# Routing of tokens to experts: maxima made earlier, running sums on TensorE, two multiplications on ScalarE and GpSimd

## The reference

```python
gate_logits = jnp.einsum('bsd,dn->bsn', x, Wg) + bg
gate_weights = jax.nn.softmax(gate_logits, axis=-1)
topv, topi = jax.lax.top_k(gate_weights, TOPK)          # 2 of 8
h = jax.nn.gelu(jnp.einsum('bsd,ndh->nbsh', x, W1) + b1[:, None, None, :], approximate=False)
h = jax.nn.gelu(jnp.einsum('nbsh,nhf->nbsf', h, W2) + b2[:, None, None, :], approximate=False)
eo = jnp.einsum('nbsf,nfd->nbsd', h, W3) + b3[:, None, None, :]
comb = jnp.sum(jax.nn.one_hot(topi, NE, dtype=x.dtype) * topv[..., None], axis=-2)
out = jnp.einsum('nbsd,bsn->bsd', eo, comb)
```

## Time and profile before

| | before |
|---|---|
| runs, us | 1767.7, 1780.8, 1783.01 |
| profiled execution, us | 1767.65 |
| its span, us | 1765.9 |
| TensorE busy | 1422.5 us, 81% |
| VectorE busy | 975.9 us, 55% |
| ScalarE busy | 614.0 us, 35% |
| GpSimd busy | 418.3 us, 24% |
| mean granted TensorE clock | 0.933 |

### The profile page before, as it was taken

One profiled execution on the slowest core, in us unless ns is written; L12 is line 12 of the kernel. 1 busy time (PEld: TensorE's weight loads), 2 busy tenths in 40 slices (PEclk: granted clock), 3 DMA queues, 4 the chain that ended last, 5 costly groups with the idle time before them and its releaser, 6 DMA issues. The chain is left out here.

```text
span 1765.9 us, 29494 instructions
## 1 busy us (share of the span) xinstructions
PE 1422.5 (81%) x9331; PEld 878.0 (50%) x9331; DVE 975.9 (55%) x2623; ACT 614.0 (35%) x1389; POOL 418.3 (24%) x588
## 2 busy tenths in 40 slices
PE   2466888888888986399999993568888875899997
PEld 1234555555555553155656562345555543566554
DVE  5456666666666652522222223367878752567775
ACT  0122444434444443022222231335555542232231
POOL 2233223322223200111111103454555420000000
PEclk9878999999999998599999996789999997899999
DMA  3245344533444310651111102664555420200000
GB/s 89 58 50 66 47 60 53 64 51 54 54 53 56 45 24 9 233 180 68 32 35 34 33 25 55 172 119 103 113 110 118 98 51 20 72 1 13 12 1 25
DMA packets 165337, 112.77 MB, mean 64 GB/s; under 512 B 32690, under 2 KB 155826, under 8 KB 165056
## 3 DMA queue, kind: packets, MB, share of 16 engines
q1 hardware_dynamic: 150272, 99.04, 27.7%
q0 software_dynamic: 3408, 9.31, 2.2%
q10 hardware_dynamic: 11504, 2.53, 0.8%
HBM read 46.48 MB, written 12.45 MB: 33 GB/s over the span
## 5 line engine op out<-in xcount | busy, mean ns | idle before, releaser
L892 ACT ACTIVATE first_probs<-pair 128x512 f32<-128x512 f32 x320 | 190.3, 597 | 302.6 <-PE pair L408 273.4
L449 DVE TENSOR_REDUCE first_negmax_x<-bank 128x2 f32<-128x512 f32 x256 | 177.0, 692 | 109.5 <-PE bank L393 96.1
L1885 ACT ACTIVATE second_probs<-pair 128x512 f32<-128x512 f32 x192 | 113.8, 598 | 129.2 <-PE pair L408 112.6
L393 PE MATMUL bank<-kept_stack_cross 96*128 96x256 bf16 x768 | 150.4, 277 | 9.7 <-DMA kept_stack_cross<-second_parts_x_q 7.9
L408 PE MATMUL pair<-kept_stack_cross 98*128 98x256 bf16 x768 | 148.8, 276 | 1.5 <-DMA kept_stack_cross<-second_rows_x 1.0
L1439 PE MATMUL pair<-kept_w,experts_hidden_t 128*128 x312 | 141.5, 596 | 0.0
L386 PE MATMUL bank<-kept_mask_q,kept_ident 128*128 128x512 bf16 x256 | 99.3, 388 | 35.0 <-DVE first_negmax_x L449 26.8
L449 DVE TENSOR_REDUCE second_negmax_x<-bank 128x2 f32<-128x512 f32 x128 | 88.5, 692 | 60.2 <-PE bank L393 52.2
L393 PEld LDWEIGHTS bank<-kept_stack_cross 96*128 96x128 bf16 x768 | 74.1, 101 | 74.3 <-issue 21.2
L1480 ACT ACTIVATE experts_hidden_t<-bank,kept_b 128x128 f32<-128x128 f32 x156 | 44.4, 367 | 187.4 <-PE bank L1414 187.4
L1394 POOL DMA_INDIRECT experts_expert_rows<-x_mid,kept_row_of x39 | 36.9, 947 | 276.4 <-PE bank L1406 250.3
(11 more groups left out here) (430 smaller groups left out, 2974.1 us busy)
## 6 DMA issues: line engine op xcount, KB each, us to landing
kept_stack_self<-first_parts_a SPq DMA_DIRECT2D x128, 64.0 KB, 5.6
kept_w<-in_L_ffn_W SPq DMA_DIRECT2D x16, 512.0 KB, 7.5
kept_w<-in_L_ffn_W SPq DMA_DIRECT2D x8, 1024.0 KB, 7.0
kept_stack_self<-second_parts_a SPq DMA_DIRECT2D x128, 64.0 KB, 3.4
kept_stack_cross<-first_parts_x_k SPq DMA_DIRECT2D x96, 64.0 KB
kept_stack_cross<-first_parts_x_q SPq DMA_DIRECT2D x96, 64.0 KB
kept_stack_cross<-second_parts_x_k SPq DMA_DIRECT2D x96, 64.0 KB
kept_stack_cross<-second_parts_x_q SPq DMA_DIRECT2D x96, 64.0 KB
```

What stands on the lines that cost most here:

```text
L393: mm = pe.matmul(out, q, k, start=mask is None, stop=True, skip_group_check=True)
L449: return dve.tensor_reduce(negmax[:, 2 * n:2 * n + 2], bank[:, :].rearrange("p (m t) -> p m t", t=D), AX.X, ALU.max, negate=True)
L892: act.activation(probs[i % RING][:, :], key_bank[i % 2][:, :], ACT.Exp, scale=att.scale).then_inc(probs_made, 1)
L1885: act.activation(probs[i % RING][:, :], key_bank[i % 2][:, :], ACT.Exp, scale=att.scale).then_inc(probs_made, 1)
```

## The change

Per batch, `keep_logits` of the first layer now also makes the maxima and their indices. In routing, the counts per expert over all batches are summed by 16 products of 8 columns that add into the same columns of a bank, and the ranks (earlier rows and earlier batches) by 16 products of 128, 120, ... 8 columns; the doubling steps go. The running ends of tiles come from an 8 x 8 comparison table, a product and a sum. The 0/1 table of tiles is kept apart as `hot`; ScalarE multiplies it by the row number, GpSimd by the batch number, both into `in_tile`. The owners' steps stand behind the second comparison by row. The shares and the integer slots are made at the start of VectorE's list in the expert stage. Kept between stages now: `best`, `best_at`, `weight`, `share` and `slot_numbers`.

```diff
@@ keep_logits, first layer
                 dve.tensor_tensor(t["logits"][:, b, :], small_bank[:, 0:NE], t["bg"][:, :], ALU.add).then_inc(logits_kept, 1)
+                dve.drain()
+                dve.max(t["best"][:, b, :], t["logits"][:, b, :])
+                dve.drain()
+                dve.max_index(t["best_at"][:, b, :], t["best"][:, b, :], t["logits"][:, b, :])
@@ route_tokens, gpsimd
+            by_tile = [P, 2, B, TILES]
+            pool.wait_ge(iotas_made, IOTAS)
+            pool.wait_ge(hot_made, 1)
+            pool.tensor_tensor(in_tile[:, 1, :, :, :], hot[:, :, :, :], ids_b[:, :, :].unsqueeze(3).broadcast_to(by_tile), ALU.mult).then_inc(ids_b_made, 1)
@@ tensor
             pe.wait_ge(chosen_made, 1)
+            for b in range(B):
+                mm = pe.matmul(ps[1][:, 0:NE], t["ones_bf"][:, :], chosen16[:, b, :], start=(b == 0), stop=(b == B - 1))
+            mm.then_inc(counted, 1)
             flat = chosen16[:, :, :].rearrange("p b e -> p (b e)")
-
-            pe.matmul(ps[0][:, 0:P], t["before16"][:, :], flat, start=True, stop=True)
-            pe.matmul(ps[1][:, 0:P], t["ones_bf"][:, :], flat, start=True, stop=True).then_inc(counted, 1)
-            pe.wait_ge(in_tile_made, 1)
+            for step in range(B):
+                mm = pe.matmul(ps[0][:, step * NE:B * NE], t["ones_bf"][:, :] if step else t["before16"][:, :], flat[:, 0:(B - step) * NE],
+                               start=(step == 0), stop=(step == B - 1), skip_group_check=True)
+            mm.then_inc(ranked, 1)
+            pe.wait_ge(ids_p_made, 1)
+            pe.wait_ge(ids_b_made, 1)
@@ scalar
-            act.activation(share[:, :], gap[:, :], ACT.Exp).then_inc(weight_made, 1)
+            act.activation(share[:, :], gap[:, :], ACT.Exp)
+            act.wait_ge(iotas_made, IOTAS)
+            act.wait_ge(hot_made, 1)
+            act.activation(in_tile[:, 0, :, :, :].rearrange("p n b c -> p (n b c)"), hot[:, :, :, :].rearrange("p n b c -> p (n b c)"), ACT.Copy, scale=ids_p[:, 0:1])\
+                .then_inc(ids_p_made, 1)
@@ vector: maxima, indices, shares and doubling steps removed (...), now
+            dve.wait_ge(iotas_made, IOTAS)
+            dve.tensor_tensor(choice[:, :, :, :], iota8[:, :].unsqueeze(1).unsqueeze(1).broadcast_to(by_choice),
+                              first_second[:, :, :].unsqueeze(3).broadcast_to(by_choice), ALU.is_equal)
+            dve.drain()
+            dve.tensor_tensor(chosen16[:, :, :], choice[:, 0, :, :], choice[:, 1, :, :], ALU.add).then_inc(chosen_made, 1)
+            dve.tensor_tensor(below[:, :, :], iota8[:, :].unsqueeze(2).broadcast_to([P, NE, NE]), iota8[:, :].unsqueeze(1).broadcast_to([P, NE, NE]), ALU.is_gt)
...
             dve.wait_ge(counted, 1)
+            dve.tensor_scalar(tiles[:, :], ps[1][:, 0:NE], float(P - 1), 1.0 / P, ALU.add, ALU.mult)
...
+            dve.tensor_tensor(before_of[:, :, :], below[:, :, :], tiles[:, :].unsqueeze(1).broadcast_to([P, NE, NE]), ALU.mult)
+            dve.drain()
+            dve.tensor_reduce(base[:, :], before_of[:, :, :], AX.X, ALU.add)
+            dve.drain()
+            dve.tensor_tensor(ends[:, :], base[:, :], tiles[:, :], ALU.add)
             dve.tensor_scalar(base[:, :], base[:, :], float(P), None, ALU.mult)
             dve.drain()
+            dve.wait_ge(ranked, 1)
+            dve.tensor_tensor(place[:, :, :], ps[0][:, 0:P].rearrange("p (b e) -> p b e", e=NE), base[:, :].unsqueeze(1).broadcast_to([P, B, NE]), ALU.add)
+            dve.drain()
+            dve.tensor_tensor(choice[:, :, :, :], choice[:, :, :, :], place[:, :, :].unsqueeze(1).broadcast_to(by_choice), ALU.mult)
+            dve.drain()
+            dve.tensor_reduce(slots[:, :, :], choice[:, :, :, :], AX.X, ALU.add)
...
+            dve.tensor_tensor(hot[:, :, :, :], iota_t[:, :].unsqueeze(1).unsqueeze(1).broadcast_to(by_tile),
+                              tile_of[:, :, :].unsqueeze(3).broadcast_to(by_tile), ALU.is_equal).then_inc(hot_made, 1)
             dve.scalar_tensor_tensor(within[:, :, :], tile_of[:, :, :], -float(P), slots[:, :, :], ALU.mult, ALU.add)
-            dve.tensor_tensor(in_tile[:, 1, :, :, :], in_tile[:, 0, :, :, :], ids_b[:, :, :].unsqueeze(3).broadcast_to(by_tile), ALU.mult)
-            dve.drain()
-            dve.tensor_scalar(in_tile[:, 0, :, :, :], in_tile[:, 0, :, :, :], ids_p[:, 0:1], None, ALU.mult).then_inc(in_tile_made, 1)
+            dve.drain()
             for n in range(2):
                 dve.tensor_tensor(in_row[:, n, :, :], iota_p[:, :].unsqueeze(1).broadcast_to(by_row),
                                   within[:, n, :].unsqueeze(2).broadcast_to(by_row), ALU.is_equal).then_inc(in_row_made, 1)
+            dve.tensor_tensor(reached[:, :, :], iota_t[:, :].unsqueeze(2).broadcast_to([P, TILES, NE]),
+                              ends[:, :].unsqueeze(1).broadcast_to([P, TILES, NE]), ALU.is_ge)
+            dve.drain()
+            dve.tensor_reduce(owner[:, :], reached[:, :, :], AX.X, ALU.add)
+            dve.drain()
+            dve.tensor_scalar(t["owner"][:, :], owner[:, :], float(NE - 1), None, ALU.min)
             dve.wait_ge(listed, 1)
@@ run_experts, vector, ahead of the first copy_rows
+            dve.tensor_reduce(total[:, :], t["weight"][:, :, :], AX.X, ALU.add)
+            dve.memset(t["slots"][:, :, B:], 0)
+            dve.tensor_copy(t["slots"][:, :, 0:B], t["slot_numbers"][:, :, :])
+            dve.drain()
+            dve.reciprocal(t["shares"][:, 0, :], total[:, :])
+            dve.drain()
+            dve.tensor_tensor(t["shares"][:, 1, :], t["share"][:, :], t["shares"][:, 0, :], ALU.mult)
             copy_rows(0)
```

More of the change, by code:

```diff
@@ L1190, in route_tokens @@
         sb, sem = open_tensors(nc, ctx, "route")
-        best, best_at = sb("best", [P, B, 8]), sb("best_at", [P, B, 8], U32)
         first_second = sb("first_second", [P, 2, B])
         less = sb("less", [P, B, NE])
-        weight = sb("weight", [P, B, NE])
-        total, gap, share = sb("total", [P, B]), sb("gap", [P, B]), sb("share", [P, B])
-        choice = [sb(f"choice_{n}", [P, B, NE]) for n in range(2)]
+        weight, share, slots = t["weight"], t["share"], t["slot_numbers"]
+        gap = sb("gap", [P, B])
+        choice = sb("choice", [P, 2, B, NE])
         chosen16 = sb("chosen16", [P, B, NE], BF16)
[L1198 to L1201, removed]
+        place = sb("place", [P, B, NE])
+        tiles, ends, base = (sb(n, [P, NE]) for n in ("tiles", "ends", "base"))
+        below, before_of = (sb(n, [P, NE, NE]) for n in ("below", "before_of"))
         iota8, iota_t = sb("iota8", [P, NE]), sb("iota_t", [P, TILES])
@@ L1262, in _ @@
         def _(dve):
[L1263 to L1271 removed]
+            logits, best, best_at = t["logits"], t["best"], t["best_at"]
+            by_choice, by_tile, by_row = [P, 2, B, NE], [P, 2, B, TILES], [P, B, P]
             for n in range(2):
@@ L1304, in _ @@
             dve.drain()
-            dve.tensor_copy(ends[:, :], tiles[:, :])
-            at, other = ends, ends2
-            for step in (1, 2, 4):
-                dve.drain()
-                dve.tensor_tensor(other[:, step:], at[:, step:], at[:, :NE - step], ALU.add)
-                dve.tensor_copy(other[:, 0:step], at[:, 0:step])
-                at, other = other, at
+            dve.tensor_tensor(before_of[:, :, :], below[:, :, :], tiles[:, :].unsqueeze(1).broadcast_to([P, NE, NE]), ALU.mult)
@@ L1312, in _ @@
             dve.drain()
-            dve.tensor_tensor(base[:, :], at[:, :], tiles[:, :], ALU.subtract)
-            dve.tensor_tensor(reached[:, :, :], iota_t[:, :].unsqueeze(2).broadcast_to([P, TILES, NE]),
-                              at[:, :].unsqueeze(1).broadcast_to([P, TILES, NE]), ALU.is_ge)
-            dve.tensor_tensor(place[:, :, :], run[now][:, :, :], counts[:, :, :], ALU.subtract)
+            dve.tensor_reduce(base[:, :], before_of[:, :, :], AX.X, ALU.add)
             dve.drain()
-            dve.tensor_reduce(owner[:, :], reached[:, :, :], AX.X, ALU.add)
+            dve.tensor_tensor(ends[:, :], base[:, :], tiles[:, :], ALU.add)
@@ L1328, in _ @@
             dve.drain()
-            for n in range(2):
-                dve.tensor_reduce(slots[:, n, :], choice[n][:, :, :], AX.X, ALU.add)
-            dve.drain()
-            dve.memset(t["slots"][:, :, B:], 0)
-            dve.tensor_copy(t["slots"][:, :, 0:B], slots[:, :, :])
             dve.tensor_scalar(tile_of[:, :, :], slots[:, :, :], 0.5 * P - 0.5, 1.0 / P, ALU.subtract, ALU.mult)
@@ L2585, in program @@
             ("wd_t", [P, KT, LAT], F32), ("absorbed_t", [P, KT, P], F32), ("wuv_t", [P, D], F32), ("wo1_t", [P, KT, D], F32),
-            ("logits", [P, B, NE], F32), ("slots", [P, 2, B + 2], I32), ("shares", [P, 2, B], F32), ("owner", [P, TILES], I32), ("row_of", [P, TILES], I32),
```

(1 more changed line is left out.)

47 lines of the change are left out of this document (8 added, 39 removed).

## The result

The changed kernel takes 1765.21 us, the median of 22 runs (1762.44 to 1774.42). The kernel before, run as often, takes 1775.43 us (1762.74 to 1784.71). The ratio is 0.9949, with a 95% interval of 0.9933 to 0.9965: some 9 us faster, between 6 and 12 (the two medians themselves lie 10.2 us apart). That is within 1%, as forecast, and on the forecast's side; but the sum said 3.1 us, and the 1777 us of the forecast are 12 us above the measured median. The profiled execution of the changed kernel took 1765.42 us (span 1763.6, mean clock 0.924), against 1767.65 (1765.9, 0.933).

The account below looks back on a forecast made before the run. Routing (26.2 of 1765.9 us) delays a TensorE-paced expert stage, so its end is paid in full. Routing -4.36, later start +0.55, first layer +0.7 give -3.1 us from the median 1780.8: about 1777 us, range 1760 to 1785.

Parts of the forecast that it names:

- the 0.55 that it adds at the end: Last batch of the first layer: its index search has no cover, so routing starts 0.55 us later.
- the hold: First comparison by row: VectorE with two SBUF inputs is blocked by GpSimd's product until 725.44, 2.41 us.
- The front: Routing's start: 3.46 us come off nominally, but almost nothing is gained, as the matmuls stand behind the b12 transposes.
- The narrow products: Routing's count and rank matmuls on TensorE: taken as 0.065 us apart, with bounds of 0.03 and 0.29.
- The 22.4 us that the prediction gives as a sign: Stage from first weight issue to first gather would take about 22.4 us instead of 26.2.
- One step came right by luck: After routing: nothing later uses up the gain, as SP has issued the first weights by 724.6, nine microseconds before the gather.
- The term for the first layer (+0.7): First layer: index searches delay reductions TensorE waits for; cost between 0 and 1.4 us, taken as 0.7.
- VectorE was held: Rival, comparisons by row: no hold between the engines, rows start at 723.03, sum -5.5 us, 1775; chance 0.2.
- GpSimd finished at 725.86 and not after the second comparison: Rival: GpSimd loses the race twice, multiplies after both comparisons by row, 727.5 to 730.0; -1.7 us, 1779; chance 0.15.
- the index search cost nothing that shows: Rival, first layer: each batch's index search delays reductions TensorE needs, up to 9.3 us; +5.5 us, 1786; chance 0.12.
- a narrow product took 0.027 us and not 0.29: Rival, routing's counts and ranks: narrow products cost 0.29 us each, slots at about 727.1; +3.4 us, 1784; chance 0.04.
- The one that the first layer moves by ten: Rival: the first layer falls into another pattern of waits and moves ten or more us either way; chance 0.1.

Follow-up runs that it names:

- experiment 3: Changed kernel with the place within the tile (`within`) in PSUM instead of SBUF; 1762.29 us, 0.9933 of the kernel before, routing 19.1 us.
- experiment 4: Changed kernel with TensorE's wait for the bias rows and their eight transposes put behind the rank products; 1760.57 us, 0.9925 of the kernel before, routing 17.6 us.
- exp. 5: Changed kernel with both `within` in PSUM and the bias transposes behind the rank products; 1762.56 us, 0.9941 of the kernel before, routing 15.5 us.
- experiment 1: Kernel before with only the maxima and indices moved to each batch's logits; 1773.12 us, 0.9994 of the kernel before.
- exp. 9: Kernel before with the changed kernel's five kept tensors allocated and unused, so later addresses shift; 1774.35 us, 0.9988 of the kernel before.
- exp. 6: Half program: kernel before without second layer and retrieval block, experts' rows copied to the output; 1090.59 us, 5 runs.
- exp. 10: Kernel before with shares and slot cast moved to the expert stage; 1772.34 us, 0.9985 of the kernel before.
- exp. 2: Changed kernel with maxima and indices put back at routing's start; 1763.67 us, 0.9938 of the kernel before.
- exp. 8: Changed kernel with 5.15 us of useless comparisons behind the slot numbers, so the gather is as late as before; 1768.47 us, 0.9968 of the kernel before.
- exp. 7: Half program: changed kernel without second layer and retrieval block, experts' rows copied to the output; 1084.6 us.
- exp. 11: Changed kernel with shares and integer slots put back into routing; 1766.99 us, 0.9952 of the kernel before.
- exp. 12: Changed kernel with both products of the tile table back on VectorE; 1766.41 us, 0.9942 of the kernel before.
- the first series: One of three series of experiments, each with its own runs of the unchanged kernel before; that kernel's median here was 1774.41 us.

## Why the prediction was right, and where it was not

Times from the first weights' issue (712.47 in the changed kernel), us; the predicted ones are those of the prediction less 711.40, without the 0.55 that it adds at the end:

| step | predicted | measured |
|---|---|---|
| index search, end of the last logits to its own end | 0.55 | 0.57 |
| counts read by VectorE | 6.2 | 5.69 |
| slot numbers ready | 9.2 | 8.73 |
| GpSimd's product starts, its length | 11.5, 2.5 | 11.12, 2.27 |
| comparison by row, free of the hold | 14.04 | 13.25 |
| gather | 21.85 | 21.08 |

The forecast held as far as it went, no change beyond 1% and a time inside 1760 to 1785 us, but that range was as wide as the spread of the runs, and the size inside it was not hit. Of the 12 us between 1777 and 1765.21, 5.4 come from the start: the median of three runs was 1780.8, that of 22 is 1775.43. The rest is the gain, too small in the sum.

**Routing held step by step.** The front gained nothing, the ranks were there before they were needed, the multiplication on GpSimd held VectorE (2.11 us, predicted 2.41), and the gather fell at 733.55, predicted 733.8. That hit has two small misses in it that cancel. The narrow products ran faster than my 0.065 us apart: sixteen of them took 0.58 us, and with 0.17 us for one that is 0.027 us apart, just under the lower bound of 0.03 that I had stated. With a shorter hold, routing is 0.8 us shorter than I said. (The 22.4 us that the prediction gives as a sign hold the 0.55 once too often, since the first weights' issue moves by it too; its own sum has 21.85.) In this trace the last logits came 0.52 us later than in the one before, in the direction of the 0.7 us that I had given the first layer.

**One step came right by luck.** The prediction says that nothing later uses the gain up, because SP has issued the first weights nine microseconds before the gather. What a gather meets is their transfer and not their issue, and the transfer lasted until about 21 us after the first issue, where the changed kernel's gather stands at 21.08. Experiments 3, 4 and 5 are what would have come of a routing 2 to 5.6 us shorter.

The Trainium skill (TensorE: Matmul & The Clock Gate, section Wait — 56ns, not 53.3ns?) gives about 25 ns as the least from start to start of small matmuls; the trace agrees, with 27 ns for sixteen products that all load the same table of ones. On the hold, the Trainium skill (SBUF — State Buffer, section Who interferes with whom) has the lock between a two-operand VectorE instruction in SBUF and GpSimd; experiment 3 agrees, and also with the way out, since no hold is left with an operand in PSUM.

**The term for the first layer (+0.7) did not show.** The reductions came late in the four batches that the prediction had named, and by more than it said, but TensorE's wait is 25.3 us against 26.0. Over the nine profiled executions with the index search in the first layer the last logits start at 709.5 us on average, over the five without it at 709.4, while single ones lie between 708.1 and 712.4. So the best figure is about 0, but with five executions on one side 0.7 is not excluded either, and experiment 1 (1.1 us less by its ratio, from 3.5 less to 1.2 more) can't tell them apart. The 0.52 us of the profiled pair is part of that spread. With 0 in place of 0.7, and the measured 26.21 - 21.08 = 5.13 off routing in place of 4.36, the sum would have been -5.13 + 0.57 = -4.6 us.

**The total was mis-sized:** -3.1 us against 9 (6 to 12). Of the 6 us of difference, 0.8 are routing's and at most 0.7 the first layer's. The other 4.5 stand in no term: the step that fell short is the one that ended the sum at the gather and took everything else to stay as it was. They are not in the traces either: the profiled pair ends 2.3 us apart, and the profiled executions of the four whole kernels with the old routing and the eight with the new average 1768.6 and 1764.5 us, 4.1 apart, about what the mended sum says. Two things about that can be shown.

First, which profile one happens to get. In the expert stage TensorE starts at a granted clock of 0.50 (1.2 GHz) and goes to 1.00 (2.4 GHz) some time later. The windows view from 741 to 751 us, first of the kernel before, then of the changed one:

```profile
741.00:746.00 5.00, 4.10 (x6) 1.18 (x4) 0.69 (x2) 0.00 (x0) 1.24 (x2) 0.50 0.76 240
746.00:751.00 5.00, 3.91 (x13) 2.08 (x14) 1.54 (x3) 1.14 (x4) 0.94 (x1) 0.97 0.79 274
```

```profile
741.00:746.00 5.00, 3.61 (x9) 1.98 (x9) 1.12 (x2) 1.14 (x4) 0.94 (x1) 0.50 0.92 319
746.00:751.00 5.00, 5.00 (x7) 1.88 (x6) 0.69 (x1) 0.00 (x0) 0.00 (x0) 0.55 0.07 21
```

Both had TensorE busy for most of those windows, and yet the kernel before is at 2.4 GHz from about 746.3 us, the changed one from about 750.5, though its first rows came 4 us earlier. Counted from TensorE's first gathered rows, all fourteen profiled executions fall into two groups:

| clock rises after | executions | first rows to last expert tile, us |
|---|---|---|
| 4.2 to 5.8 us | before 5.7, exp. 1 4.2, exp. 9 5.6, exp. 6 5.8 | 326.6 on average |
| 13.4 us | exp. 10 | 327.4 |
| 4.2 to 4.9 us | exp. 2 4.2, exp. 4 4.4, exp. 8 4.9 | 324.3 on average |
| 13.1 to 13.8 us | after 13.8, exp. 3 13.7, exp. 5 13.1, exp. 7 13.4, exp. 11 13.2, exp. 12 13.8 | 328.6 on average |

The upper two rows are kernels with the old routing, the lower two with the new. With the new one, executions with a late rise are 4.3 us longer; with the old one the only such execution is 0.8 us longer, so the price of a late rise is not settled. The profiled pair compares an early rise with a late one, and gives back 1.5 us of the 5.1 gained in routing (326.5 us from first rows to last tile before, 328.0 after). Experiment 2, with the same routing and an early rise, came to its last tile at 1058.1 us against 1067.1, 9 us earlier, but its span was only 4.7 us shorter: what follows the experts took 703.0 us there and 698.7 before. Over the twelve whole kernels that rest lies between 698.0 and 703.0 us, on average 700.3 with the old routing and 699.9 with the new, so the traces show no gain behind the experts.

Second, where the profiled executions stand among the runs. Those of four kernels with the old routing lie 2.5 to 7.8 us under the medians of their own runs (5.2 on average; the one of before took 1767.65 against a median of 1775.43, and against 1774.41 in the first series). Those of the eight with the new routing lie between 3.7 us under and 4.6 over theirs, 0.0 on average. A gain taken from traces is short by the difference, 5.2 us. That all four lie low is hardly a draw: of 90 recorded executions of the kernel before, 12 are as fast as the slowest of these four.

**What stays open** is what the unprofiled runs of the kernel before do in those 4 to 5 us. It was neither the shares (11), nor the work on the other two engines (12), nor the earlier gather alone (8); the addresses (9) could hold a part. The clock's rise is a candidate: with an early rise on both sides the gain would be 4.6 from routing and 326.6 - 324.3 = 2.3 behind it, 6.9 us, inside the interval; with a late rise on both sides it would be 4.6 - 1.2 = 3.4, outside it. But only profiled executions show when it rises. The mean clocks of the unprofiled runs, 0.9220 over 73 with the new routing and 0.9198 over 101 with the old, lean towards more time at the full clock without saying where. The halves (5.1 us by the ratios, 4 either way) leave room for a part in the second layer too.

Of the rivals, none came true. VectorE was held, GpSimd finished at 725.86 and not after the second comparison, the index search cost nothing that shows, and a narrow product took 0.027 us and not 0.29. The one that the first layer moves by ten did not come either: the last logits start at 710.50 against 709.98.

## What to carry to other kernels

A short serial stage between two long ones is where a chain counted step by step holds to within a microsecond; what such a gain becomes behind it depends on a transfer (here a weight prefetch that fills the DMA engines) and on when the clock rises, so shorten it only until the next transfer is the bound. Before giving VectorE's work to GpSimd, compare the whole GpSimd duration with what VectorE saves, unless an operand of the VectorE instruction beside it can be in PSUM. And one profiled execution is one out of a spread of 20 us, and need not lie in its middle: for a gain of 0.3% compare medians of many runs, and look in which group the profile fell before reading a difference of a few us out of a pair.

The version to try next is that of experiment 4, 0.9925 of the kernel before: one block of eight transposes moved behind the narrow products. Its rows arrive 1.1 us earlier than the changed kernel's, but its interval (0.9904 to 0.9946) overlaps the other (0.9933 to 0.9965), so six runs do not show that it is faster.

## What the runs showed of the hardware that was not expected

- Sixteen products of 8 columns, bf16, each with its own load of the same 128 x 128 table, took 0.58 us at a granted clock of 0.50, and their sixteen weight loads 0.50 us.
- A gather of one tile's rows took 3.0 to 3.1 us from issue to use when the DMA engines were mostly idle (share 0.13 to 0.33), and 4.9 to 5.9 us with the share at 0.73 to 1.05.
- A GpSimd product of 1248 bf16 elements took 2.27 us, whether it overlapped a VectorE comparison with both inputs in SBUF (held for 2.11 us) or one with an input in PSUM (not held).
- The same expert stage reached the full clock either 4.2 to 5.8 or 13.1 to 13.8 us after its first matmul, in seven executions each, and never in between.
